# One turn of a feed-forward pipeline: two PSUM copies ahead of a normalisation, a constant read from PSUM, and two small factors computed in common instructions

## Reference

```
x1  = layernorm(x + s_o * (softmax(q k' / 4) v) w_o' + b_o)
q4(x): scale = max(max|block| / 6, 1e-12); nearest of (0, .5, 1, 1.5, 2, 3, 4, 6) * sign * scale
h   = silu(q4(x1) q4(w_gate)') * (q4(x1) q4(w_up)')
out = layernorm(x1 + q4(h) q4(w_down)')
```

## Time and profile before

| | us |
|---|---|
| median of three executions | 1951.57 (1950.83 to 1952.59) |
| the profiled execution's own time | 1952.79 |
| its span, first to last instruction | 1950.9 |
| PE busy / DVE busy / ACT busy / POOL busy in the span | 1917.4 / 1829.3 / 1640.8 / 965.9 |
| of these, DVE and POOL from 1443 to 1819 us (376 us) | 358.2 and 239.6 |
| DVE and POOL from 1819 to 1909 us (90 us) | 87.8 and 75.9 |

### The profile page before, as it was taken

One profiled execution on the slowest core, in us unless ns is written; L12 is line 12 of the kernel. 1 busy time (PEld: TensorE's weight loads), 2 busy tenths in 40 slices (PEclk: granted clock), 3 DMA queues, 4 the chain that ended last, 5 costly groups with the idle time before them and its releaser, 6 DMA issues.

```text
span 1950.9 us, 43533 instructions
## 1 busy us (share of the span) xinstructions
PE 1917.4 (98%) x16042; PEld 1114.7 (57%) x16042; DVE 1829.3 (94%) x3088; ACT 1640.8 (84%) x3226; POOL 965.9 (50%) x833
## 2 busy tenths in 40 slices
PE   8999999999999999999999999999999999999998
PEld 7776444444444444444444444444478888888876
DVE  4798999999999999999999999998299999999997
ACT  5655999999999999999999999998967777777776
POOL 3000446675776765466232223323156666666785
PEclk9999999999999999999999999999999999999999
DMA  7985633455354445335444643543112211211210
GB/s 224 303 261 212 115 59 47 79 100 116 79 115 102 95 94 116 100 79 110 106 95 92 117 101 79 110 106 111 50 52 66 66 66 66 66 66 55 66 41 28
DMA packets 134976, 195.64 MB, mean 100 GB/s; under 512 B 38700, under 2 KB 83500, under 8 KB 134764
## 3 DMA queue, kind: packets, MB, share of 16 engines
q1 hardware_dynamic: 127084, 185.26, 38.4%
q10 hardware_dynamic: 7392, 7.34, 1.2%
q0 software_dynamic: 288, 0.27, 0.1%
HBM read 110.76 MB, written 80.48 MB: 98 GB/s over the span
## 4 chain that ended last, share of the span: by engine, by line
DVE 62%; PE 33%; issue 3%; ACT 1%; DMA 0%; DVEq 0%; SPq 0%; POOLq 0%; POOL 0%; ACTq 0%
DVE halfmax L1172 43%; DVE halfmax L1167 14%; PE ps L1478 10%; PE ps L1517 6%; PE ps L512 4%; PE ps L524 2%; PE ps L1082 2%; PE ps L1466 2%; PE ps L1489 2%; PE ps L1048 1%; PE ps L1534 1%; PE ps L499 1%; PE ps L1525 1%; DVE room L1668 1%; PE ps L1023 1%
## 5 line engine op out<-in xcount | busy, mean ns | idle before, releaser
L1133 ACT ACTIVATE room<-ps 128x512 f32<-128x512 f32 x2048 | 1086.2, 600 | 104.6 <-PE ps L1048 79.7
L1172 DVE TENSOR_REDUCE halfmax<-ps 128x1 f32<-128x512 f32 x1470 | 900.1, 674 | 0.0
L1048 PE MATMUL ps<-qs,ks 50*128 50x512 f32 x2048 | 718.9, 448 | 2.5 <-DVE halfmax L1172 1.2
L1023 PE MATMUL ps<-ks,qs 48*128 48x512 f32 x1960 | 678.4, 439 | 4.6
L1082 PE MATMUL ps<-room,vals 128*17 128x256 f32 (+2 forms) x8192 | 578.1, 384 | 0.2 <-ACT craw L1141 0.2
L1023 PEld LDWEIGHTS ps<-ks,qs 48*128 48x128 f32 x1960 | 311.4, 184 | 406.8 <-DVE halfmax L1172 250.0
L1048 PEld LDWEIGHTS ps<-qs,ks 50*128 50x128 f32 x2048 | 324.9, 184 | 19.5 <-ACT room L1133 13.8
L1082 PEld LDWEIGHTS ps<-room,vals 128*17 128x17 f32 x8192 | 167.4, 96 | 251.2 <-issue 186.7
L164 POOL CAST mrow<-turned_rows 128x32 fp32r<-128x32 f32 x32 | 6.7, 208 | 605.7 <-DVE turned_rows L159 605.7
L1167 DVE TENSOR_REDUCE halfmax<-ps 128x2 f32<-128x1024 f32 x245 | 295.2, 1205 | 0.9 <-PE ps L1023 0.8
L1478 PE MATMUL ps<-wguT,xqT 128*128 128x512 f32 (+1 forms) x1152 | 266.4, 384 | 4.2 <-DVE xqT L1708 4.2
(11 more groups left out here) (129 smaller groups left out, 2316.5 us busy)
## 6 DMA issues: line engine op xcount, KB each, us to landing
qk_parts<-parts SPq DMA_DIRECT2D x64, 512.0 KB, 4.8
qs<-qk_parts SPq DMA_DIRECT2D x192, 128.0 KB, 4.3
ks<-qk_parts SPq DMA_DIRECT2D x192, 128.0 KB, 6.7
ctx_raw<-craw SPq DMA_DIRECT2D x64, 256.0 KB
ready<-passing_half SPq DMA_DIRECT2D x27, 512.0 KB, 5.0
pairs<-ready SPq DMA_DIRECT2D x27, 512.0 KB, 3.6
out_dram<-fin SPq DMA_DIRECT2D x64, 128.0 KB, 1.7
passing<-ctx_raw SPq DMA_DIRECT2D x58, 128.0 KB
```

What stands on the lines that cost most here:

```text
L1023: nc.tensor.matmul(ps[:, MX + max_number(i, u, bank) % 4, :], qs[rows, i.slot(RING), pair, t * P:(t + 1) * P], ks[rows, i.slot(RING), pair ...
L1048: nc.tensor.matmul(ps[:, score_bank(i, s, n), :], ks[rows, slot, pair, kt * P:(kt + 1) * P], qs[rows, slot, pair, qh * BANK:(qh + 1) * BAN ...
L1133: nc.scalar.activation(prob[:, prob_slot(i, s), score_order(i, s)[n], :], ps[:, score_bank(i, s, n), :], ACT.Exp, scale=float(D) ** -0.5). ...
L1172: nc.vector.tensor_reduce(halfmax[:, i.slot(2), bank, column:column + 1], ps[:, at + bank, :], AX.X, ALU.max, negate=True).then_inc(max_re ...
```

## The change

Three edits, all in `feed`.

1. ACT. `x1_normal` is split into `x1_shift` (wait for the factor, L1553, L1554) and the normalisation L1572, and `copy_hT` into the copies of pieces 4 and 5 and `copy_rest`. The order becomes shift, pieces 4 and 5, normalisation, rest.
2. DVE. In step 0 the floor is copied once to 60 columns of PSUM bank WO, and `scale` reads it there. So that PE does not write that bank while DVE reads the floor, the output projection of each tile from the third on waits for one more semaphore, `grid_chain`.
3. POOL. The factor of x1's norm for tile k-1 and that of the second norm for tile k-8 are computed together in step k, each instruction on 128x2 in place of two on 128x1. The pair at the end of the step goes (but for the drain's steps).

```
@@ output_projection
+                if t.k == 0:
+                    pe.wait_ge(sems["floor_ready"], 1)
+                if t.k >= 2:
+                    pe.wait_ge(sems["grid_chain"], scaled(t.k))
@@ scalar
-        def x1_normal(t):
-            due(act, "rstd1_ready", t.lin(1, 1))
-            shift(t, 0, 0, "shift1_chain")
+        def x1_shift(t):
+            act.wait_ge(sems["rstd_ready"], first_rstd[t.k])
+            shift(t, 0, 0, "shift1_chain")
+        def x1_normal(t):
             due(act, "z_used", t.lin(1, 1 - U))
...
+        def copy_rest(t):
             act.wait_ge(sems["hT_psum"], t.lin(2, 2))
...
-            for lag, stage in ((3, copy_xqT), (9, output), (2, bend_x), (4, bend_h), (3, silu), (1, x1_normal),
-                               (5, copy_hT)):
+            for lag, stage in ((3, copy_xqT), (9, output), (2, bend_x), (4, bend_h), (3, silu), (1, x1_shift),
+                               (5, copy_hT), (1, x1_normal), (5, copy_rest)):
@@ scale
-                                                in1=numbers[:, 2:3].to_broadcast([P, top.shape[1]]), op0=ALU.mult,
+                                                in1=floor[:, 0:top.shape[1]], op0=ALU.mult,
@@ vector
+            if i.k == 0:
+                nc.vector.tensor_copy(floor, numbers[:, 2:3].to_broadcast([P, NBH + NBX])).then_inc(sems["floor_ready"], 1)
@@ gpsimd
-            power(t, 0, "pow1_chain", "rstd1_ready")
+            for k1, k2 in norms(i.k):
+                power(k1, k2)
...
+            nc.gpsimd.tensor_tensor(rstd[:, at, 0:1], mv[:, at, 1:2], number(0), ALU.add).then_inc(sems["var_ready"], 1)
+            pool.wait_ge(sems["var_ready"], done[0])
+            nc.gpsimd.tensor_tensor(rstd[:, at, 1:2], rstd[:, at, 0:1], number(1), ALU.pow).then_inc(sems["rstd_ready"], 1)
...
-            t = i.plus(-7)
...
-                power(t, second(t), "pow2_chain", "rstd2_ready")
```

More of the change, by code:

```diff
@@ L1371, in feed @@
     z = take(2, H)
-    names = ("xb_ready ctx_ready wo_psum wo_used mv1_ready rstd1_ready "
+    names = ("xb_ready ctx_ready wo_psum wo_used mv1_ready rstd_ready "
              "x1_ready xsum_ready xgrid_ready xq_ready xt_psum xqT_high xqT_ready xn_ready xm_ready xbend_ready hn_ready hm_ready hbend_ready gate_psum up_psum silu_ready h_made "
-             "hsum_ready hgrid_ready hq_ready hT_psum hT_ready dn_read dn_psum z_used mv2_ready rstd2_ready fin_ready "
-             "stats1_ready stats2_ready grid_chain pow1_chain pow2_chain shift1_chain shift2_chain last_ready").split()
+             "hsum_ready hgrid_ready hq_ready floor_ready hT_psum hT_ready dn_read dn_psum z_used mv2_ready fin_ready "
+             "stats1_ready stats2_ready grid_chain var_ready shift1_chain shift2_chain last_ready").split()
     sems = {name: sem(name) for name in names}
@@ L1380, in feed, with norms, last_norms, scaled @@
     second = lambda t: 1 + t.slot(2)
+    def norms(k):
+        if 1 <= k <= NT:
+            return [(k - 1, k - 8 if k >= 8 else None)]
+        return [(None, NT - 7)] if k == NT + 1 else []
+    def last_norms(k):
+        return [(None, k - 7)] if NT + 1 <= k < NT + 7 else []
+    first_rstd, second_rstd = {}, {}
+    for count, (t1, t2) in enumerate((pair for k in range(TILES_RUN) for pair in norms(k) + last_norms(k)), 1):
+        if t1 is not None:
+            first_rstd[t1] = count
+        if t2 is not None:
+            second_rstd[t2] = count
     x_across = ps[:, HT + 1, H:2 * H]
+    floor = ps[:, WO, H:H + NBH + NBX]
+    def scaled(k):
+        return 3 * (k - 2) + 2 if k < 4 else 6 + 4 * (k - 4) + 3
     def due(eng, name, n):
@@ L1559, in output @@
                 return
-            due(act, "rstd2_ready", t.lin(1, 1))
+            act.wait_ge(sems["rstd_ready"], second_rstd[t.k])
             shift(t, 1, second(t), "shift2_chain")
@@ L1677, in vector @@
         for i in each(ks):
+            if i.k == 0:
+                nc.vector.tensor_copy(floor, numbers[:, 2:3].to_broadcast([P, NBH + NBX])).then_inc(sems["floor_ready"], 1)
+            if i.k == 2:
+                dve.wait_ge(sems["floor_ready"], 1)
             if i.k == RDEN_IN:
@@ L1724, in vector @@
                 due(dve, "stats1_ready", t1.lin(1, 1))
-                due(dve, "rstd1_ready", t1.lin(1))
+                if t1.k > 0:
+                    dve.wait_ge(sems["rstd_ready"], first_rstd[t1.k - 1])
                 nc.vector.bn_aggr(mv[:, 0], stats[:, 0]).then_inc(sems["mv1_ready"], 1)
@@ L1761, in vector @@
             if t7.k == NT - 1:
-                due(dve, "rstd2_ready", t7.lin(1, 1))
+                dve.wait_ge(sems["rstd_ready"], second_rstd[t7.k])
                 wait(dve, stored[t7.slot(2)], t7.turn(2, 16))
@@ L1767, in gpsimd, with power @@
     def gpsimd(pool, ks):
[L1768 to L1774, removed]
+        done = [0]
+        def power(k1, k2):
+            n = [0] if k2 is None else [1 + k2 % 2] if k1 is None else [0, 1 + k2 % 2]
+            at = slice(n[0], n[-1] + 1, max(n[-1] - n[0], 1))
+            done[0] += 1
+            if k1 is not None:
+                due(pool, "mv1_ready", k1 + 1)
+                due(pool, "x1_ready", k1)
+            if k2 is not None:
+                due(pool, "mv2_ready", k2 + 1)
+                due(pool, "fin_ready", k2 - 1)
+            number = lambda c: numbers[:, c:c + 1].unsqueeze(2).to_broadcast([P, len(n), 1])
+            nc.gpsimd.tensor_tensor(rstd[:, at, 0:1], mv[:, at, 1:2], number(0), ALU.add).then_inc(sems["var_ready"], 1)
+            pool.wait_ge(sems["var_ready"], done[0])
+            nc.gpsimd.tensor_tensor(rstd[:, at, 1:2], rstd[:, at, 0:1], number(1),
+                                    ALU.pow).then_inc(sems["rstd_ready"], 1)
         for i in each(ks):
@@ L1809, in gpsimd @@
                                         ALU.mult).then_inc(sems["hq_ready"], 1)
-            t = i.plus(-7)
-            if t.ok(NT):
-                due(pool, "mv2_ready", t.lin(1, 1))
-                due(pool, "fin_ready", t.lin(1, -1))
-                power(t, second(t), "pow2_chain", "rstd2_ready")
+            for k1, k2 in last_norms(i.k):
+                power(k1, k2)
     return Programs(sync, gpsimd, tensor, scalar, vector)
```

## The result

The changed kernel takes 1954.7 us (median, 1952.5 to 1959.2), the kernel before, measured beside it, 1952.0. The ratio is 1.0013, 95% interval 1.0007 to 1.0019: the change makes the kernel slower, by 2.7 us between the medians. The forecast was 1951.3, a gain of 0.3. The measured time lies in the forecast's range, but on the other side of the kernel before.

The account below looks back on a forecast made before the run. A loop through PE and ACT was taken to bind the middle part, DVE the raw steps. Middle +1.6, raw -0.1, filling -1.2, draining -0.6 sum to -0.3: 1952.5 against the profiled 1952.79, 1951.3 us on the median; range 1947.2 to 1955.4.

Parts of the forecast that it names:

- That is PE's only wait in the turn: Middle part: PE waits only at L1534, for ACT's copy of piece 5 in odd steps, 0.10 us a turn.
- The bound of the gain, -2.3 us: Middle part, best case: gate and semaphore wait cost nothing and PE's 0.10 us a turn is gained.
- The third semaphore costs 0.06: PE's projection: waiting for three semaphores takes 0.17 in place of 0.117 us, 0.06 more, on the loop in even steps.
- L1572, 0.51 to the one behind it: ACT, odd step: the rest copy starts 0.51 us after x1's normalisation L1572, a term of the loop.
- slower rival: ACT, odd steps: piece 5 holds two instructions, rest copy 0.11 later, loop 16.50, 1953.8 or 1954.8 us; chance 0.15.
- The gate, 0.41: ACT: piece 4 can start only 0.41 us after L1489's first matmul, PE's turning of h; ACT loses 0.06.
- The loop: Middle part: closed loop through PE and ACT, 16.39 against 16.32 us a turn, +1.6 us over 23 turns.
- Floor: DVE: L1646 reading the floor from PSUM takes 0.21 us everywhere, -0.27 per collision, nothing in the middle part.
- POOL: POOL: two-column power takes 0.16 us longer; middle part 0, raw part in all -0.1 us.
- Filling, -1.2: Filling: L1675 goes ahead of the later L1794, -0.35 in two steps, and two L1646 collisions go, about -0.25 each.
- Draining, -0.6: Draining: two more L1646 collisions on the chain go, and 0.05 at the rest copy: -0.6 us.
- floor rival: DVE: L1646 still collides with its floor in PSUM, in all +3.1, 1954.7 us; chance 0.04.

Follow-up runs that it names:

- e4: Changed kernel with x1's normalisation behind all three copies of turned h on ACT: 1943.9 us, ratio 0.9963.
- e1: Kernel before with only the order on ACT changed, floor and POOL's factors as they were: 1956.5 us, ratio 1.0023.
- e3: Changed kernel with the two small copies swapped, piece 5 ahead of piece 4: 1947.2 us, ratio 0.9978.
- e5: Kernel before with the floor in PSUM alone (its copy, PE's third semaphore, L1646's new input): 1948.0 us, ratio 0.9980.
- e7: Changed kernel, unaltered, profiled once more: 1952.4 us in that one execution.
- e8: Kernel before, unaltered, profiled once more: 1957.0 us in that one execution.

## Why the prediction was wrong, by its own steps

- **"That is PE's only wait in the turn"** failed. I took L1534's 0.41 against 0.31 us as the whole wait, as if 0.31 were its length undisturbed; that is 0.22. The wait was 0.28 us a turn, and the even step's part of it stood in the trace of before (L1534 0.14 us behind L1588's end, as in the odd step). The bound of the gain, -2.3 us, was too narrow: -6.8 was there in the middle part (e4), for an order that keeps x1 out of the way of the rest copy.
- **"The third semaphore costs 0.06"** failed. What I read as its price in the earlier trace rows, 0.17 in place of 0.117, was PE's wait for ACT in the even step, the 0.09 above in part. In the changed kernel PE goes from the first L1518 to the first L1495 in 0.57 us with three semaphores as with two before, and L1563, with three of its own, starts 0.12 after the last L1495.
- **"L1572, 0.51 to the one behind it"** failed: it is 0.62 in odd steps. This is the step that failed for the order on ACT. The second held instruction, given as the slower rival with a chance of 0.15, is shown by runs: it stands in e1, is gone in e3 when only the order of two copies is changed, and is absent in the even steps of all, where piece 5 has 64 rows too but begins at row 0. The Trainium skill ("VectorE: DVE Perf Modes", Two Vector instructions with no wait between them) gives this rule for Vector instructions, SBUF and PSUM apart; the rows show ScalarE behaving by it.
- **The gate, 0.41,** is 0.47 in the middle part, in every variant that reaches it. Why the drain shows less stays open.
- The loop as measured: 0.47 + 0.29 + 0.30 + 0.62 + 0.60 + 0.05 to the third matmul + 0.10 more to the fourth + 14.03 = 16.46; 14.03 is what is left of the turn. The forecast was 16.39. That it came so near is in part luck: ACT's terms were 0.20 too small (second hold 0.11, gate 0.06, small copies 0.03), and PE's were 0.13 too large (the semaphore 0.06, and 14.10 had the even step's unseen wait in it). Without the 0.11 of the second hold the measured terms give 16.35, still above before. That an earlier piece 5 doesn't help when the rest copy is wanted next was right; of +2.9 us in the middle part +1.6 was forecast.
- **Floor:** right in its price, 0.21 everywhere, and in being worth nothing in the middle part's turn; e5 gains 0.4 us over the middle part.
- **POOL:** right in its prices. L1822 0.89 against 0.73, L1707 1.18 against a forecast of 1.17, raw steps 8.61 against 8.63. The first raw step gained 0.6 where 0.4 was forecast. What I did not draw from it is that the change would be 2 us better without this part.
- **Filling, -1.2,** failed for a reason in the code: `norms` takes the second factor in only from step 8 on, so while the pipeline fills the power has one column, L1840 is not later and L1707 does not go first. L1707 still takes 1.24 us there. Only L1678's collisions went, -0.24 and -0.18 in two steps, and the next one gave 0.09 back; e5, with the floor alone, has the same two gains.
- **Draining, -0.6:** right (-0.5).

In short, the mechanism of the floor and of POOL held, and the sign was lost in the loop through ACT, +2.9 in place of +1.6 (the rest copy's second hold, 0.62 for 0.51 us), and in the filling, -0.3 in place of -1.2 (a second column that isn't there yet). The slower rival had the mechanism and a turn of 16.50. The floor rival's 1954.7 is the measured median by chance: its own condition, an L1678 that still collides, did not come.

## What to carry to other kernels

When an instruction is moved ahead of another, ask what the consumer wants next: here the small copies came early, and the big one, wanted 0.43 us after the first matmul that reads a small one, stayed behind the same three instructions. Keep partition offsets in mind where an order is written: in these runs an ACT instruction on rows 64 to 127 cost its followers their overlap, once for SBUF and once for PSUM, so put one that uses both memories right behind it (e3). And measure an engine's own pace from a variant in which it never waits, or set each start against the end of what it waits for in every step, before calling a wait its only one.

## What the hardware showed that I had not expected

- ACT's x1 and the copies around it overlap by about 0.10 us (0.49 us from the start of x1 to that of the next, x1 lasting 0.59) unless the operand in SBUF or in PSUM last began at another partition: then 0.62. The rest copy is held although x1, which touches SBUF alone, stands between it and piece 5; so it is PSUM's side that still counts there. Only row 64 against row 0 was measured.
- PE's granted clock falls to half (1.2 of 2.4 GHz) after the same gap of 2.07 us in 6 of 14 profiles, though PE's starts in the 7 us before it are the same within 0.01 us in all. The fall costs 0.9 us in the filling (8.67 to 8.69 in place of 7.78 us). What decides it is open. Others of these stretches lie in the last 60 us of attention. Two profiled executions of one kernel differed by about 4 us (e7 and e8 against the first ones).
